# A graph kernel on one core: VectorE's chain and assembling of a unit are put ahead of both variances

## The reference, cut to what matters

```
def _L1_gnn_ref(x, edge_index, W, b, gamma, beta, num_rounds):
    ...
    deg = jax.ops.segment_sum(jnp.ones_like(dst, dtype=x.dtype), dst, num_segments=n)
    dis = jnp.where(deg > 0, jax.lax.rsqrt(deg), 0.0)
    norm = dis[src] * dis[dst]
    for _ in range(num_rounds):
        h = x @ W
        msgs = h[src] * norm[:, None]
        agg = jax.ops.segment_sum(msgs, dst, num_segments=n) + b
        mu = agg.mean(axis=-1, keepdims=True)
        var = agg.var(axis=-1, keepdims=True)
        x = (agg - mu) * jax.lax.rsqrt(var + EPS) * gamma + beta
    return x
...
x = _layernorm(x + _L1_gnn_ref(x, edge_index, ..., 4), axis=-1)
```

## Time and profile before

| | us |
|---|---|
| median of three runs | 10540.99 |
| lowest and highest | 10538.47, 10543.46 |
| the profiled execution | 10568.15 |
| its span | 10566.3 |
| r1a, r1b (4833 to 5363, 5363 to 5895) | 530, 532 |
| r2 (5911 to 6480), not changed | 569 |
| r3 (6485 to 7035) | 550 |
| r4 (7047 to 8086) | 1039 |

### The profile page before, as it was taken

The page is one execution under the profiler, slowest core; times in us unless marked ns, Lnnn a source line. Parts: engine busy times, 40 slices in busy tenths (PEclk is TensorE's granted clock), DMA queues, the critical chain, the costliest instruction groups (busy, mean ns, idle before and its releaser), DMA issues. The chain is left out here.

```text
span 10566.3 us, 116038 instructions
## 1 busy us (share of the span) xinstructions
PE 5778.3 (55%) x28479; PEld 4118.1 (39%) x28479; DVE 6794.6 (64%) x14079; ACT 2812.3 (27%) x5049; POOL 7336.9 (69%) x7144
## 2 busy tenths in 40 slices
PE   3756999400000000776867786767774668833338
PEld 1453333100000000775656565555553557733326
DVE  8954333385878787996767676878775766622227
ACT  0042222100222222443434453222221332200006
POOL 2654777577777777775767676767776767677764
PEclk9978999755555555887777787777676775555559
DMA  0064333143545454446866676655444999811127
GB/s 14 4 221 137 71 72 74 31 160 115 166 147 166 148 166 151 121 129 163 223 196 221 194 236 197 228 179 146 137 134 119 316 270 116 115 46 46 45 55 278
DMA packets 1350058, 1518.83 MB, mean 144 GB/s; under 512 B 935889, under 2 KB 1057071, under 8 KB 1349818
## 3 DMA queue, kind: packets, MB, share of 16 engines
q1 hardware_dynamic: 1088840, 1253.58, 37.1%
q0 software_dynamic: 252192, 248.44, 13.5%
q10 hardware_dynamic: 8786, 14.21, 0.4%
HBM read 852.44 MB, written 795.02 MB: 156 GB/s over the span
## 5 line engine op out<-in xcount | busy, mean ns | idle before, releaser
L2600 POOL DMA_INDIRECT r_got<-state,comb_src x1176 | 1197.9, 1019 | 367.6 <-issue 349.5
L314 POOL DMA_INDIRECT payload_or_bias_rows<-payload,place x784 | 875.0, 1116 | 483.6 <-issue 254.4
L1816 PE MATMUL hop_ps_into<-hop_out,span_s 128*128 128x256 f32 x8 | 4.9, 714 | 2047.2 <-DVE hop_out L1644 2047.2
L1453 POOL DMA_INDIRECT hop_got<-edges_b,next_col x784 | 825.7, 1053 | 261.6 <-issue 236.3
L1453 POOL DMA_INDIRECT hop_got<-edges_a,next_col x784 | 782.1, 998 | 259.7 <-issue 238.4
L1816 PEld LDWEIGHTS hop_ps_into<-hop_out,span_s 128*128 128x128 f32 x8 | 2.0, 311 | 2049.5 <-DVE hop_out L1644 2049.5
L1712 ACT COPY hop_got<-hop_zeros 128x1792 f32<-128x1792 f32 x224 | 378.2, 1688 | 1107.4 <-DVE hop_ps_msg L1595 1098.6
L1644 DVE SCALAR_TENSOR_TENSOR hop_out<-hop_out,hop_runs_now,hop_ps_msg 128x256 f32<-128x256 f32 x1176 | 565.6, 481 | 51.3 <-DVE hop_ps_msg L1597 0.5
L2882 PE MATMUL r_ps_v<-dense1g,r_gt 128*128 128x128 f32 x3136 | 570.1, 353 | 0.0
L2882 PEld LDWEIGHTS r_ps_v<-dense1g,r_gt 128*128 128x128 f32 x3136 | 516.4, 256 | 127.0 <-issue 127.0
L2700 DVE SCALAR_TENSOR_TENSOR r_acc<-r_acc,r_runs_now,r_got 128x64 f32<-128x64 f32 x1173 | 335.1, 286 | 289.9 <-DMA r_got<-state,comb_src 251.1
(11 more groups left out here) (842 smaller groups left out, 18108.8 us busy)
## 6 DMA issues: line engine op xcount, KB each, us to landing
edges_a<-hop_out SPq DMA_DIRECT2D x112, 896.0 KB
edges_b<-hop_out SPq DMA_DIRECT2D x112, 896.0 KB, 4.3
r_in<-state SPq DMA_DIRECT2D x168, 448.0 KB, 4.6
hop_side<-x_dst SPq DMA_DIRECT2D x280, 224.0 KB, 4.5
own<-plain_y SPq DMA_DIRECT2D x56, 952.0 KB
x_and_sums<-c_y SPq DMA_DIRECT2D x56, 896.0 KB, 5.9
last_in<-x_and_sums SPq DMA_DIRECT2D x56, 896.0 KB
r1a_in<-own SPq DMA_DIRECT2D x84, 448.0 KB, 6.1
```

Source lines behind the costliest of these rows:

```text
L314: nc.gpsimd.indirect_dma_start(out=t.raw[:, n, :], out_offset=None, in_=t.pay[k], in_offset=bass.IndirectOffsetOnAxis(t.place[:, k, n:n + ...
L1453: pool.indirect_dma_start(out=got[:, u, c, :], out_offset=None, in_=table, in_offset=at, bounds_check=EP - 1, oob_is_err=False).then_inc(g ...
L2600: pool.indirect_dma_start(out=got[:, n, c - b * CT, :], out_offset=None, in_=table, in_offset=bass.IndirectOffsetOnAxis(idx[:, at + c:at + ...
```

## The change

The table that sets the order of DVE's work in a turn is written with the front first, and the special case for r2, which had that order already, goes.

```diff
             @staged(dve, steps, units, JOIN)
             def _(ago):
-                order_of_work = ((NORM, variance), (JOIN, r_variance), (0, front), (JOIN, r_norm), (NORM, norm))
-                if keeps:
-                    order_of_work = ((0, front), (NORM, variance), (NORM, norm))
+                order_of_work = ((0, front), (NORM, variance), (JOIN, r_variance), (JOIN, r_norm), (NORM, norm))
                 for lag, work in order_of_work:
                     for i, u in ago(lag):
                         work(i, u)
```

## The result

The changed kernel takes 10555.8 us in the median of 20 runs, the kernel before 10539.8 in 20 runs beside it: a ratio of 1.0017 with a 95% interval of 1.0010 to 1.0023, so 10 to 24 us slower. One of the changed kernel's 20 runs took 11108 at a granted clock of 0.589 instead of 0.70; it is left out of the ratio. Predicted was 10542, with 10527 to 10558. The time is inside that range and under the 0.2% that was called no change. But the interval excludes zero, and the forecast of +0.6 missed a real cost of about 16 to 18.

A forecast was written before the change was run, and what follows sets the result against it. POOL's issue of gathers and scatters was taken to bound all four passes; terms of 1.0 + 0 - 0.4 + 0 = +0.6 on the median of 10540.99 gave 10542, range 10527 to 10558.

The forecast's parts named there:

- All four passes run at POOL's pace; POOL's pauses stay at 0.3.: In r1a, r1b, r3 and r4 POOL waits for no one; each pause before a gather or scatter is its own issue.
- r1a and r1b steady, period 34.4, nothing gained.: DVE's period per chunk stays 34.4, below POOL's 35.8; two root bubbles (0.56) are paid with PE's transposes.
- Rival 1: DVE falls behind POOL in r1a and r1b through ACT's queue: period 37.5, +48, 10590; chance 7%.
- r1a's tail +1.0: Last front of r1a can't start earlier; from it to PE's next product 7.96 becomes 8.97.
- r1b's tail 0: Last front of r1b starts about 1.0 earlier and is followed by 1.0 more; -1.0 to +1.0 possible.
- r3: -0.4: End of r3: front starts 3.1 earlier, L2772 comes 2.7 later behind it; ends -1.8 and +2.7.
- the steady part gains nothing: In r3 DVE's loop becomes 16.45, below POOL's 18.05 as before, so the pass keeps POOL's pace.
- r4: 0: r4 unchanged: its end is the last scatter, and in the steady part 7.77 of waiting covers 2.7.
- the cover: At r4's end, 15.4 us between DVE being done and the last chunk's scatters, against a delay of some 3 to 5.
- POOL's stretch: POOL's busy time over 0.94 a gather and 0.98 a scatter in the four passes, 91 in all; given no term.
- rival 2: DVE's order changes the gathers' issue time: a third less of 91 is -30, 10511, a third more the same upward; 5%.

The follow-up runs named there:

- e1: The new order in r1a and r1b alone, r3 and r4 keeping the old one: 10545.7 against 10550.4 for the kernel before, ratio 1.0002.
- e4: The changed kernel with six scalar_tensor_tensor made tensor_tensor: 10574.1, ratio 1.0019 against the kernel before.
- e8: The changed kernel with L2772, L2774, L2777 and L2812's factor in PSUM in r3 and r4, and r2 without its SBUF copy: 10519.2, ratio 0.9983 to the kernel before.
- e11: The kernel before, old order, with L2772, L2774, L2777 and L2812's factor in PSUM in r3 and r4: 10556.9, ratio 1.0016.

## Why the prediction was right in its range and wrong in its step

*All four passes run at POOL's pace; POOL's pauses stay at 0.3.* Right, in every window.

*r1a and r1b steady, period 34.4, nothing gained.* Right. Two fronts of half 0, with no wait for gathers at the second, are now at 5218.18 and 5252.53, 34.35 apart. Roots are waited for 0.28 in turns with a front as well (97 times in r1a, 66 before). e1 shows no difference either. Rival 1 is out.

*r1a's tail +1.0.* The step held, and the tail did not lengthen. From the last front to PE's product it is 5336.45 - 5327.52 = 8.93, forecast 8.97:

```profile
5327.52 0.62 DVE L2690 SCALAR_TENSOR_TENSOR r1a_got<-r1a_got 128x448 f32<-128x448 f32 x1 [0.35 <-DMA r1a_got<-own,t_row_s]
...
5336.45 0.90 PE L2877 MATMUL r1a_ps_v<-brow,ones 3*128 3x512 bf16 x2 [1.06 <-DVE r1a_y L2787]
...
5340.57 1.86 PE L2874 MATMUL r1a_ps_v<-bt,r1a_rows_now 28*128 28x512 f32 x4
5342.37 1.83 PE L2880 MATMUL r1a_ps_v<-dense,r1a_gt 128*128 128x128 f32 x14
```

Behind it PE ran its T product at the higher of its two levels (1.86 and 1.83; at the lower one the same instructions take 3.35 and 3.36, as in the kernel before at 5347.86 and 5351.14), and the tail came out 2.0 shorter. Over the other kernels r1a and r1b together took 1070.9 to 1081.6 in either order, so a term of 1 can't be seen there.

*r1b's tail 0.* It became 1.1 shorter. The front was waited for (1.07, data-bound, 2.44 behind the start of the last gather instead of 5.17), so DVE's row gained 2.7 and not 1.0; behind it PE's product comes 8.93 later instead of 7.35.

*r3: -0.4.* The pieces hold. The wait for the square is gone (36.1 before in 23 times, 2.3 once after), that for gathers grew, both roots bubble:

```profile
DVE r_acc L2700 <- DMA r_got<-state,comb_src: 67.6, 26, 10.5
...
DVE r_stat L2767 <- ACT r_stat L2910: 8.2, 29, 0.3
DVE r_rstat L2801 <- ACT r_rstat L2915: 7.9, 28, 0.3
```

At the end L2772 comes 7004.40 - 6996.66 = 7.74 behind the front instead of 4.96, +2.8, forecast +2.7. The front started 4.85 behind the last issue's end, before 6.10, so 1.25 were won where I took 3.1: the gathers landed late again, and the blank rows' stores are not the reason, since the last chunk has none. So L2772 came 1.5 later behind the last issue than before. The tail stayed at 53.8 all the same, because one of PE's products behind it ran at the higher level, 1.83 instead of 3.35 for the same 14 instructions. Before and after:

```profile
7012.28 3.35 PE L2882 MATMUL r_ps_g<-gw,r_gt 128*128 128x128 f32 x14
...
7010.29 1.83 PE L2880 MATMUL r_ps_g<-gw,r_gt 128*128 128x128 f32 x14
```

So the tail's -0.2 agrees with the forecast of -0.4 by luck: the front gave 1.25 and not 3.1, and PE's clock, which had no term, gave the rest. What failed in r3 is the sentence that the steady part gains nothing: it lost 7.3.

*r4: 0.* The tail is 13.9 in both, the cover held. The steady part lost 7.0.

**The step that failed** is the one that gave POOL's stretch no term: "the same instructions meet the same gathers, only 3 to 6 us shifted". A shift of a few us against a cycle of 1.245 is everything, since the price of a meeting goes from 0 to 0.9 with the place where the issue falls in it. It was the upward half of rival 2, given 5% and a third of the stretch of 91 either way; 14 came, a sixth. (The 5% was then counted as faster, though the rival was priced both ways.) The measured time lies inside the range in part by luck: the range allowed a tenth of the stretch, 9, and the rest of its upper side, 7, was meant for the ends and the spread of the runs. The step was within reach. The 0.94 of most gathers and the 1.24 in the earlier trace rows could have been set beside the DVE row they lay under. On the rule: the section that I cited from the Trainium skill (SBUF — State Buffer, "Who interferes with whom") has a second clause, that a VectorE instruction with two SBUF inputs contends with a GpSimd instruction that reads SBUF. I weighed only the clauses on copies and reduces. An issue here reads its row numbers from SBUF (`comb_src`, `put_t`), and the trace agrees with the clause (1.33 beside L2812). The same section of the Trainium skill takes descriptor writing to be spared by a tensor_tensor, as an inference; here the issue as a whole is not spared (1.32 in e4, whose tensor_tensor held as much as its other form). Whether the reading or the writing waits no run separates. The section's sentence that issue order decides who blocks agrees with the trace on POOL's side alone (below).

## What to carry to other kernels

Where a queue of equal, back-to-back DMA issues sets the pace, its own mean duration is a term of the sum: take the shortest duration as the floor, list what runs on VectorE under each longer one, and look at the distance between two such instructions before and after any change of order. Move one operand of a big elementwise instruction to PSUM where it came from there anyway; in r4 that won 32 us against the changed kernel and 25 against the kernel before, more than any order did. Check first that holding the PSUM bank longer doesn't bind the loop (e8, e11).

## What was not expected of the hardware

**A cliff at the start.** In the traces of before, after and e1 to e4, every issue that starts 0.046 us or more after the start of a big instruction with two SBUF inputs (and before its last tenth) is held; none that starts within 0.038 is (0.94 to 1.02), and between the two both occur. In the second case the DVE instruction pays a little instead, 1.12 to 1.17 for 1.09. It pays next to nothing for an issue that is under way already: of the 922 that started in before and after more than 0.02 behind an issue's start and under it, none took over 1.10. In r4 before, L2777 is mostly in that place:

```profile
7689.48 1.14 DVE L2777 SCALAR_TENSOR_TENSOR r_r<-r_v,r_x 128x896 f32<-128x896 f32 x1
7689.49 0.98 POOL L2608 DMA_INDIRECT x<-r_yt,put_t  x1 [0.30 <-issue]
```
